# Three edge passes of a graph network: each 128-edge tile gathered once and found by registers

## The chip, the cores and the metric

The kernel runs on one core of a Trainium2 chip. The metric is the device time of one execution, in microseconds, as the median of several runs. One further execution was taken with the hardware profiler, and all rows come from that one.

## What is computed

A graph has 6250 nodes of 256 features and 100,000 edges, sorted by destination. Node numbers of destinations go as the square of a uniform number, so the first nodes have many edges each and the last ones few. Three attention steps run over the edges, with dense node work between them (cut from the reference):

```
layer 0, GAT, 4 heads:  logits = leaky_relu(a_src[src] + a_dst[dst]); alpha = softmax of logits over each dst
                        x1 = prelu(segment_sum(h[src] * alpha, dst) + bias)
layer 0, attention:     logits2 = sum(q[d2] * k[s2]) * scale; alpha2 = softmax over each d2
                        out = prelu(segment_sum(v[s2] * alpha2, d2) + x1 @ Wskip + bskip)
layer 1, typed GAT, 8 heads: alpha = leaky(xs[src] . a_s[etype] + xd[dst] . a_d[etype]); softmax over dst, times edge weight
                        out = segment_sum(xs[src] * a, dst) + bias; layernorm, feed-forward, layernorm
```

## The kernel before, in words

The program is a chain of stages with a barrier between them: `visits_and_nodes_in`, an edge pass ("gat"), `nodes_mid`, an edge pass ("attn", with `ph.dot` true), `nodes_between`, an edge pass ("typed"), `nodes_ffn`. The three edge passes are one function, `edge_pass`, called with three `Phase` objects; I call them passes one, two and three.

The 100,000 edges are cut into NT = 782 tiles of 128 edges, the 6250 destinations into 49 blocks of 128 nodes. A **visit** is a tile together with one destination block that it touches. A tile on the border of two blocks is visited twice, so there are 782 + 48 = 830 visits, filled up to VISIT_END = 832, in 52 **batches** of G = 16.

For each visit GpSimd issues one indirect DMA (line 278) that gathers the source rows of the tile's 128 edges from a table in HBM into a ring X of 48 (pass two: 40) slots in SBUF. The row numbers come from column 0 of `m.tables`, which SyncE loads batch by batch. TensorE spreads destination data over the edges through a one-hot matrix (`expand`, line 374 in pass two, 378 in the others). In passes one and three VectorE adds source and destination parts of the logits for a whole batch (`source_logits`, line 469 or 466, at the start of a batch and one batch ahead), runs a chain of scans for the running maximum of each destination, and then scales each gathered tile by its weights in place (`scale_rows`, line 591). In pass two VectorE forms a dot product per visit 25 visits ahead (`dot`, line 454), and ScalarE makes weighted one-hots (lines 307 and 313). In all passes TensorE sums a visit into PSUM (line 425), and VectorE adds that to the block's accumulator (line 613), whose place comes from a register. `rescale` (line 599 in pass two, 603 otherwise) shrinks the accumulator at a batch's start.

Order is written out by hand. Each engine runs one loop over v, with the work of each visit at fixed offsets, and semaphores between them. In VectorE's loop the order at v is: scale v + 2 (or dot v + 25), chain parts, add v - 1, more chain parts. A scaling waits until the add just before it has finished:

```
                if v >= 4:
                    dve.wait_ge(S["added"], v - 3)
                row = X[:, v % RING, 0:D].rearrange("p (h c) -> p h c", h=H)
```

VectorE loads the 16 block numbers of a batch into registers by one load per batch (line 444), TensorE four numbers per load (line 356). SyncE issues all loads of tables, one-hots, segments and joins, and waits there for buffers to come free. VectorE itself waits for gathered tiles (`landed`, in `dot` and `source_logits`), by groups of QUARTER = 4 visits. GpSimd does nothing in a pass but the gathers.

## Time and profile before

| | |
|---|---|
| median of 3 runs | 4141.51 us (4139.8 to 4142.21) |
| the profiled execution's own time | 4127.7 us |
| its span, first to last instruction | 4126.1 us |
| TensorE busy | 3059.6 us, 74% |
| VectorE busy | 3194.5 us, 77% |
| ScalarE busy | 1535.4 us, 37% |
| GpSimd busy | 2771.6 us, 67% |
| mean granted TensorE clock | 0.858 |
| first gather of passes one, two, three, at | 141.7, 1384.2, 2626.7 us |
| last gather of passes one, two, three, at | 1182.6, 2423.9, 3667.6 us |

The span is the stretch that the trace covers. "Busy" leaves out register, branch, semaphore and DMA-issuing instructions, but counts GpSimd's indirect gathers. The letter q behind an engine's name (DVEq, PEldq, SPq) stands for its sequencer, which fetches instructions, waits for semaphores and does register work. A row of the timeline gives start (us), length (us), engine, line, operation, operands and, in brackets, the engine's idle time just before and what ended it. A row of windows gives the stretch and its length, the busy us (and instructions) of TensorE, TensorE's weight loads, VectorE, ScalarE and GpSimd, the granted TensorE clock, the busy share of the DMA engines and GB/s.

### The profile page before, as it was taken

Reading aid. Unit: us, or ns where it says so; the run is one execution under the profiler, and the core shown is the slowest. Engines: PE = TensorE matmul, PEld = TensorE weight load, DVE = VectorE, ACT = ScalarE, POOL = GpSimd, SP = SyncE. Lnnn points to the kernel's source line nnn. Section 1 sums busy time; section 2 is a strip of 40 time slices with the busy share of each in tenths; the row PEclk is TensorE's granted clock in tenths of the full one; section 3 lists DMA queues with packets and bytes.
Section 4 is the critical chain, followed back from the end, with each engine's and each line's share of the span. In section 5 each row is a group of like instructions: output and inputs, shape, how many; then the busy total and the mean of one; then the engine's idle time right before and its main releaser. Section 6 shows DMA issues by size and latency. Waiting matters only on the chain. (4 is left out here: it accounts for less than half of the span.)

```text
span 4126.1 us, 67495 instructions
## 1 busy us (share of the span) xinstructions
PE 3059.6 (74%) x15494; PEld 2152.1 (52%) x15494; DVE 3194.5 (77%) x11152; ACT 1535.4 (37%) x3947; POOL 2771.6 (67%) x3112
## 2 busy tenths in 40 slices
PE   6467677766667688778788779577777777768998
PEld 4344445444446455455555546344444444447887
DVE  6577888777787677777777769688888888887665
ACT  2333333333328466666666656211111111113332
POOL 3577777777730477777777745677777777746776
PEclk8778887788879799999999989788788888789999
DMA  7655555555534444444444436555555555532221
GB/s 144 176 168 166 167 167 168 170 173 168 167 82 131 137 136 140 139 137 137 137 137 137 139 96 221 186 157 159 156 157 156 156 159 160 152 85 89 66 66 46
DMA packets 297058, 586.64 MB, mean 142 GB/s; under 512 B 89485, under 2 KB 186777, under 8 KB 296746
## 3 DMA queue, kind: packets, MB, share of 16 engines
q0 software_dynamic: 123184, 355.57, 31.4%
q1 hardware_dynamic: 141434, 197.50, 16.0%
q10 hardware_dynamic: 32128, 29.99, 2.4%
q8 instruction: 126, 2.06, 0.2%
q14 instruction: 186, 1.52, 0.1%
HBM read 505.09 MB, written 77.73 MB: 141 GB/s over the span
## 5 line engine op out<-in xcount | busy, mean ns | idle before, releaser
L425 PE MATMUL psum<-big,onehots_or_distances 128*128 128x264 f32 (+2 forms) x4992 | 1885.5, 488 | 149.7 <-ACT onehots_or_distances L313 86.2
L613 DVE TENSOR_TENSOR acc<-acc,psum 128x264 f32 (+2 forms) x2496 | 1062.8, 426 | 259.1 <-PE psum L425 153.5
L425 PEld LDWEIGHTS psum<-big,onehots_or_distances 128*128 128x128 f32 x4992 | 937.1, 228 | 433.3 <-issue 167.7
L278 POOL DMA_INDIRECT big<-table_attn,tables x832 | 787.4, 946 | 453.8 <-DMA tables<-edge_tables 200.7
L278 POOL DMA_INDIRECT big<-table_typed,tables x832 | 788.7, 948 | 264.3 <-issue 194.6
L278 POOL DMA_INDIRECT big<-table_gat,tables x832 | 788.7, 948 | 263.7 <-issue 187.4
L334 ACT ACTIVATE onehots_or_distances<-psum 128x512 f32<-128x512 f32 x416 | 248.6, 597 | 1630.9 <-PE psum L388 1570.4
L591 DVE TENSOR_TENSOR big<-big,psum 128x256 f32<-128x256 f32 x1664 | 679.7, 414 | 26.9 <-ACT psum L299 1.4
L378 PE MATMUL psum<-big 128*128 x1664 | 279.4, 196 | 453.5 <-DVE raw L479 228.1
L374 PE MATMUL psum<-big,onehot_t 128*128 x2496 | 456.0, 294 | 113.9 <-DVE raw L454 102.0
L454 DVE CUSTOM_DVE_ANT_0 junk<-psum,big 128x258 f32<-128x258 f32 x832 | 346.2, 417 | 197.4 <-DMA big<-table_attn,tables 185.8
L378 PEld LDWEIGHTS psum<-big 128*128 128x128 bf16 x1664 | 187.3, 114 | 591.2 <-issue 520.7
L307 ACT ACTIVATE onehots_or_distances<-iota,tables 128x128 f32<-128x128 f32 x832 | 330.5, 397 | 386.7 <-DVE acc L613 376.8
L374 PEld LDWEIGHTS psum<-big,onehot_t 128*128 128x128 bf16 x2496 | 258.1, 104 | 305.4 <-issue 184.6
L313 ACT ACTIVATE onehots_or_distances<-onehots_or_distances,weight,neg_weight 128x128 f32<-128x128 f32 x832 | 397.6, 478 | 0.0
L388 PEld LDWEIGHTS psum<-ident,big 128*128 128x128 bf16 x1664 | 157.6, 116 | 102.9 <-issue 44.0
L1698 ACT ACTIVATE big<-psum,big 128x128 f32<-128x128 f32 x392 | 106.7, 383 | 258.2 <-PE psum L1737 258.2
L400 PE MATMUL psum<-growth,ones 64*128 64x4 f32 (+2 forms) x312 | 63.2, 272 | 180.5 <-DVE growth L566 180.5
L388 PE MATMUL psum<-ident,big 128*128 128x128 bf16 x1664 | 196.4, 252 | 0.0
L1737 PEld LDWEIGHTS psum<-big 128*128 128x128 f32 x1568 | 186.6, 195 | 5.9 <-ACT big L1690 3.4
L1737 PE MATMUL psum<-big 128*128 128x128 f32 x1568 | 187.1, 279 | 2.8 <-ACT big L1690 2.8
L773 POOL TENSOR_TENSOR big<-big,half 128x1 f32<-128x1 f32 x147 | 101.7, 692 | 117.5 <-DVE big L768 113.7
(265 smaller groups left out, 3959.8 us busy)
## 6 DMA issues: line engine op xcount, KB each, us to landing
big<-visit_positions SPq DMA_DIRECT2D x52, 512.0 KB
onehots<-big SPq DMA_DIRECT2D x52, 512.0 KB
onehot_t<-onehots SPq DMA_DIRECT2D x52, 512.0 KB
big<-onehots SPq DMA_DIRECT2D x52, 512.0 KB, 3.7
big<-table_gat,tables POOLq DMA_INDIRECT x832
big<-table_attn,tables POOLq DMA_INDIRECT x832
big<-table_typed,tables POOLq DMA_INDIRECT x832
big<-in_x_dram SPq DMA_DIRECT2D x98, 128.0 KB, 2.4
```

Of the source, the lines that this page charges most:

```text
L278: pool.indirect_dma_start(X[:, v % RING, :], None, ph.table, bass.IndirectOffsetOnAxis(ap=column(k, 0)[:, g:g + 1].bitcast(I32), axis=0)). ...
L307: nc.scalar.activation(m.dist[:, v % 4, :], m.iota[:, :], ACT.Abs, scale=-1.0, bias=column(k, 1)[:, g:g + 1]).then_inc(S["distance"], 1)
L313: nc.scalar.activation(m.onehots[:, v % 4, :], m.dist[:, v % 4, :], ACT.Relu, scale=m.neg_weight[:, k % 2, g:g + 1], bias=m.weight[:, k % ...
L334: nc.scalar.activation(m.onehots[:, at:at + 4, :], turned_onehots.rearrange("p (v n) -> p v n", n=P), ACT.Copy).then_inc(S["onehots"], 1)
L374: last = nc.tensor.matmul(ps[:, exp_banks[v % 3], 0:K], spreading, ph.tab[:, bass.ds(blk, 1), s, :].rearrange("p a k -> p (a k)"), start=( ...
L378: last = nc.tensor.matmul(expanded_at(g), spreading, ph.tab[:, bass.ds(blk, 1), :, :].rearrange("p a s k -> p (a s k)"), start=True, stop= ...
L388: last = nc.tensor.matmul(turned_onehots[:, i * P:(i + 1) * P], onehot_t(k)[:, g * P:(g + 1) * P], m.ident16[:, :], start=True, stop=True)
L425: nc.tensor.matmul(sum_ps(v), onehot_at(v), X[:, v % RING, 0:ph.WS], start=True, stop=True).then_inc(S["summed"], 1)
L454: nc.vector.tensor_tensor_reduce(out=m.junk[:, v % 3, 0:K], in0=ps[:, exp_banks[v % 3], 0:K], in1=X[:, v % RING, 0:K], scale=1.0, scalar=0 ...
L591: nc.vector.tensor_tensor(row, row, spread(row_weights[:, g, :], D // H), ALU.mult).then_inc(S["scaled"], 1)
L613: nc.vector.tensor_tensor(row, row, sum_ps(v), ALU.add).then_inc(S["added"], 1)
L1737: last = nc.tensor.matmul(ps[:, 2 + 2 * (p % 2) + f // 4, (f % 4) * P:(f % 4 + 1) * P], w1_t[:, c, f * P:(f + 1) * P], uT[:, p % 2, c * P: ...
```

## The change

Each tile is gathered once: 782 gathers a pass and not 832. The visits find their tile by a ring slot that is held in a register. Its parts:

- GpSimd walks over tiles t, with row numbers from `m.src`, which stays in SBUF for the whole program. The ring has 44 slots. Before every fourth gather GpSimd waits for the semaphore `freed`.
- SyncE no longer issues loads in a pass. It waits for each group of four tiles to land, adds to a semaphore `arrived`, and, nine groups behind, waits for the last visit of a group and adds to `freed`. So a group's gathers start only after the group two before it has landed.
- ScalarE takes over the loads that SyncE issued (`transfers`), at fixed places of its loop. In passes one and three it also copies the columns behind the 256 features of each visit's tile to a buffer `m.tails` (`copy_tails`, 31 visits ahead), after it has waited for `arrived`.
- VectorE reads `m.tails` in `source_logits`, scales from the ring slot into a second ring Y of 32 visits, and loads 16 slots per batch in addition to the 16 block numbers. In pass two its dot product reads the slot by register and doesn't wait for the landing.
- TensorE in pass two waits for `arrived` before it expands each fourth visit, 26 visits ahead, and loads four slots per four visits for its sums.
- A table of blocks, slots, needed tiles and last visits is made in the first stage. The tables of passes one and three have 260 and 272 columns, before 264 and 288.
- `tensor_tensor_reduce` in `dot` becomes `scalar_tensor_tensor` with the same accumulator output.

```diff
+RING = 44
+YR = 2 * G
+LAG = 9
...
+    def slots_of(engine, v, n):
+        at = v // G * RECORD + v % G
+        return nc.values_load_multi_w_load_instructions(
+            m.index[32:33, at:at + n], engines=[engine], min_val=0, max_val=RING - 1,
...
+            for q in range(NTQ):
+                f = q - LAG
+                last = None
+                if 0 <= f < NTQ - groups:
+                    last = sp.value_load(m.index[64:65, f:f + 1], min_val=1, max_val=VISIT_END)
+                sp.wait_ge(S[f"rows{q % groups}"], 16 * (q // groups * QUARTER + min(QUARTER, NT - q * QUARTER)))
+                sp.sem_inc(S["arrived"], QUARTER)
+                if last is not None:
+                    sp.wait_ge(S["summed" if ph.dot else "scaled"], last)
+                    sp.sem_inc(S["freed"], 1)
+
+        @block.gpsimd
+        def _(pool):
+            for t in range(NT):
+                if t >= RING and t % QUARTER == 0:
+                    pool.wait_ge(S["freed"], t // QUARTER - groups + 1)
+                pool.indirect_dma_start(X[:, t % RING, :], None, ph.table,
+                                        bass.IndirectOffsetOnAxis(ap=m.src[:, t:t + 1], axis=0)).then_inc(S[f"rows{t // QUARTER % groups}"], 16)
...
+            def copy_tails(v):
+
                 k, g = divmod(v, G)
-                if g == 0:
-                    pool.wait_ge(S[f"tables{k % TB}"], (k // TB + 1) * 16)
-                if v >= RING:
-                    pool.wait_ge(S["summed"], v - RING + 1)
...
+                if g == 0 and k >= 2:
+                    act.wait_ge(S["with_high"], k - 1)
+                if g % QUARTER == 0:
+                    act.wait_ge(S["arrived"], needs[g // QUARTER])
+                nc.scalar.activation(tails_at(k)[:, g, :], X[:, bass.ds(slots[g], 1), D:D + T].rearrange("p a w -> p (a w)"), ACT.Copy).then_inc(S["tails"], 1)
...
                 if ph.dot:
+                    if v % QUARTER == 0:
+                        pe.wait_ge(S["arrived"], need_of(PE_ENGINE, v)[0])
                     if v >= 3:
                         pe.wait_ge(S["dotted"], v - 2)
...
-                    nc.tensor.matmul(sum_ps(v), onehot_at(v), X[:, v % RING, 0:ph.WS], start=True, stop=True).then_inc(S["summed"], 1)
+                    if ph.dot and v % 4 == 0:
+                        slots = slots_of(PE_ENGINE, v, 4)
+                    rows = tile_at(slots[v % 4], ph.WS) if ph.dot else Y[:, v % YR, :]
+                    nc.tensor.matmul(sum_ps(v), onehot_at(v), rows, start=True, stop=True).then_inc(S["summed"], 1)
...
-                row = X[:, v % RING, 0:D].rearrange("p (h c) -> p h c", h=H)
-                nc.vector.tensor_tensor(row, row, spread(row_weights[:, g, :], D // H), ALU.mult).then_inc(S["scaled"], 1)
+                row = tile_at(slots[g], D).rearrange("p (h c) -> p h c", h=H)
+                nc.vector.tensor_tensor(Y[:, v % YR, 0:D].rearrange("p (h c) -> p h c", h=H), row, spread(row_weights[:, g, :], D // H), ALU.mult).then_inc(S["scaled"], 1)
...
+                u = v + (DOT_AHEAD if ph.dot else 1)
+                if 0 <= u < VISIT_END and u % G == 0:
+                    slots = ()
+                    slots = slots_of(DVE_ENGINE, u, G)
```

Three places show how the instructions now stand. ISA is a register operation of the sequencer. The first is VectorE in pass three, from the last adds of a batch over the next batch's first source logits. Before (L613 add, L579 edge weights, L591 scaling, L466 source logits, L444 block numbers):

```order
L613 ISA
L613 TENSOR_TENSOR acc<-acc,psum 128x272
L579 TENSOR_TENSOR psum<-psum,tables 128x128
L591 TENSOR_TENSOR big<-big,psum 128x256 x2
L613 ISA
L613 TENSOR_TENSOR acc<-acc,psum 128x272
L591 TENSOR_TENSOR big<-big,psum 128x256
L466 TENSOR_TENSOR both<-big,psum 128x256
L444 TENSOR_LOAD blocks
L613 ISA
L613 TENSOR_TENSOR acc<-acc,psum 128x272
```

And with the change (L663 add, L629 edge weights, L641 scaling):

```order
L663 ISA
L663 TENSOR_TENSOR acc<-acc,psum 128x272
L227 TENSOR_LOAD index
L629 TENSOR_TENSOR psum<-psum,tables 128x128
L641 ISA
L641 TENSOR_TENSOR big<-big,psum 128x256
L641 ISA
L641 TENSOR_TENSOR big<-big,psum 128x256
L663 ISA
L663 TENSOR_TENSOR acc<-acc,psum 128x272
L641 ISA
L641 TENSOR_TENSOR big<-big,psum 128x256
```

A second register load, L227, now stands before the edge weights, and every scaling has a register operation in front of it.

The second is TensorE in pass two, where a group of four visits begins. Before (L374 expand, L425 sum):

```order
L425 MATMUL psum<-big,onehots_or_distances 128x258
L356 TENSOR_LOAD blocks
L374 ISA
L374 MATMUL psum<-big,onehot_t 128x258
L374 ISA
L374 MATMUL psum<-big,onehot_t 128x258
L374 ISA
L374 MATMUL psum<-big,onehot_t 128x258
L425 MATMUL psum<-big,onehots_or_distances 128x258
```

With the change (L403 block numbers, L233 needed tile, L423 expand, L477 sum):

```order
L403 TENSOR_LOAD index
L233 TENSOR_LOAD index
L233 ISA x2
L423 ISA
L423 MATMUL psum<-big,onehot_t 128x258
L423 ISA
L423 MATMUL psum<-big,onehot_t 128x258
L423 ISA
L423 MATMUL psum<-big,onehot_t 128x258
L477 ISA
L477 MATMUL psum<-big,onehots_or_distances 128x258
```

and further on, at the first sum of a group of four:

```order
L227 TENSOR_LOAD index
L477 ISA
L477 MATMUL psum<-big,onehots_or_distances 128x258
```

Expanding now stands behind one more register load and two register operations, with the wait for `arrived` on the first L423. The sum reads its tile's place from a register, and one in four has a load in front.

The third is ScalarE in pass three with the change, behind the exponentials of a batch (L317 copies tails, L370 copies one-hots, L298 and L299 are the loads of segments and joins, L227 and L237 load slots and needs). Before, nothing stood there but the copy of the one-hots:

```order
L317 ACTIVATE dot_products<-big 128x16
L298 DMA seg<-visit_segments 128x1x385
L299 DMA joins<-visit_joins 4x128
L317 ISA
L317 ACTIVATE dot_products<-big 128x16
L370 ACTIVATE onehots_or_distances<-psum 128x512
L227 TENSOR_LOAD index
L237 TENSOR_LOAD index
L237 ISA x8
L317 ISA
L317 ACTIVATE dot_products<-big 128x16
L317 ISA
```

Two DMA issues, tail copies and the register loads now stand in ScalarE's queue between the exponentials and later copies of one-hots.

## Rows read from the trace of the kernel before

**Rows 1.** Windows in steady parts of passes one, two, three (columns below).

```profile
300.00:1100.00 800.00, 558.29 (x2707) 387.55 (x2706) 631.32 (x2185) 267.01 (x359) 605.33 (x640) 0.80 0.57 169
1500.00:2300.00 800.00, 637.84 (x3362) 416.18 (x3360) 598.14 (x2605) 499.12 (x1402) 605.01 (x641) 0.94 0.49 138
2700.00:3500.00 800.00, 581.04 (x2711) 381.85 (x2710) 698.07 (x2313) 127.16 (x279) 605.37 (x640) 0.82 0.56 157
```

**Rows 2.** Gathers of pass three by line: min/median/max ns, first and last start.

```profile
L278 POOL DMA_INDIRECT big<-table_typed,tables x832: 942/946/1131, 2626.7 to 3667.6; - x167
```

**Rows 3.** Batch cadence by line: first source-logit addition of passes one and three.

```profile
L469 DVE TENSOR_TENSOR raw<-big,psum x52: 253/261/265, 163.5 to 1186.9; 128x64 f32<-128x64 f32 x52
...
L466 DVE TENSOR_TENSOR both<-big,psum x52: 414/422/423, 2648.5 to 3671.9; 128x256 f32<-128x256 f32 x52
```

**Rows 4.** Waits of VectorE at 200:1180, 1400:2420, 2650:3660 us; total us, times, longest.

```profile
DVE raw L469 <- DMA big<-table_gat,tables: 79.0, 27, 5.5
DVE acc L613 <- PE psum L425: 69.4, 124, 1.9
DVE acc L613 <- issue: 34.9, 31, 2.1
...
DVE junk L454 <- DMA big<-table_attn,tables: 184.9, 103, 4.5
...
DVE acc L613 <- PE psum L425: 46.4, 90, 1.1
DVE both L466 <- DMA big<-table_typed,tables: 38.0, 37, 8.1
DVE acc L613 <- issue: 33.0, 39, 1.1
```

**Rows 5.** Register loads by line, on the sequencers of VectorE and TensorE.

```profile
L444 DVEq TENSOR_LOAD <-blocks x156: 1092/1099/2333, 183.4 to 3691.0; - x156
...
L356 PEldq TENSOR_LOAD <-blocks x624: 325/332/1832, 138.9 to 3661.8; - x156
```

**Rows 6.** Timeline of VectorE in pass three, round one batch boundary.

```profile
2803.42 0.43 DVE L613 TENSOR_TENSOR acc<-acc,psum 128x272 f32 x1
2803.89 0.42 DVE L591 TENSOR_TENSOR big<-big,psum 128x256 f32<-128x256 f32 x1
2804.23 0.43 DVE L613 TENSOR_TENSOR acc<-acc,psum 128x272 f32 x1
...
2808.98 0.42 DVE L466 TENSOR_TENSOR both<-big,psum 128x256 f32<-128x256 f32 x1 [0.67 <-DMA big<-table_typed,tables]
2810.26 0.44 DVE L613 TENSOR_TENSOR acc<-acc,psum 128x272 f32 x1 [0.85 <-issue]
```

**Rows 7.** Timeline of VectorE in pass two; then the rescaling line on its sequencer.

```profile
1903.37 0.42 DVE L613 TENSOR_TENSOR acc<-acc,psum 128x258 f32 x1 [0.78 <-issue]
1904.01 0.44 DVE L599 TENSOR_SCALAR acc<-acc,shrink  x1 [0.21 <-DVE acc L613]
...
L599 DVEq FUSED_REGOPS  x52: 57/57/65, 1422.3 to 2440.9; - x52
```

**Rows 8.** Waits of TensorE at 1400:2420 us; total us, times, longest.

```profile
PE psum L374 <- DVE raw L454: 94.2, 57, 3.2
PE psum L425 <- ACT onehots_or_distances L313: 83.7, 206, 1.1
```

**Rows 9.** Timeline of a gather on GpSimd and the product that waited, pass two.

```profile
1903.38 0.95 POOL L278 DMA_INDIRECT big<-table_attn,tables  x1 [0.30 <-issue]
...
1908.18 0.43 DVE L454 CUSTOM_DVE_ANT_0 junk<-psum,big 128x258 f32<-128x258 f32 x1 [2.38 <-DMA big<-table_attn,tables]
```

**Rows 10.** Timeline at the start of pass three, GpSimd and the SyncE queue.

```profile
2624.45 0.81 SPq L227 DMA_DIRECT2D tables<-edge_tables  x2
2626.68 1.07 POOL L278 DMA_INDIRECT big<-table_typed,tables  x1 [11.23 <-DMA tables<-edge_tables]
```

**Rows 11.** Timeline of ScalarE in pass three.

```profile
2805.87 0.22 ACT L292 ACTIVATE psum<-psum,first_hot 128x8 f32<-128x8 f32 x1
```

More of the change, by code:

```diff
@@ L132, with __init__ @@
 class Phase:
-    def __init__(self, m, name, heads, table, width, summed, keys, ring):
+    def __init__(self, m, name, heads, table, width, summed, keys):
         self.name, self.H, self.R = name, heads, heads * G
@@ L150 @@
 LEAD = 2 * G
-QUARTER = 4
 TB = 5
@@ L157, in edge_pass @@
 def edge_pass(nc, m, dram, ph):
-    H, R, X, K, RING = ph.H, ph.R, ph.X, ph.keys, ph.ring
+    H, R, X, Y, K, T = ph.H, ph.R, ph.X, ph.Y, ph.keys, ph.tails
     RQ = max(R, 32)
@@ L198, in onehot_t, with scaled_at, tails_at, tile_at @@
     def onehot_t(k):
-        return m.onehot_t[:, k % 2, :] if ph.dot else m.hot_ring.bitcast(BF16)[:, k % HOT, :]
+        if ph.dot or k % HOT >= 4:
+            return m.onehot_t[:, k % 2, :]
+        return m.hot_ring.bitcast(BF16)[:, k % HOT, :]
     turned_onehots = ps[:, 7, 0:4 * P]
-    def rows_at(k):
-        at = k * G % RING
-        return X[:, at:at + G, :]
+    def scaled_at(k):
+        return Y[:, k % 2 * G:(k % 2 + 1) * G, :]
+    def tails_at(k):
+        return m.tails[:, k % 2, :, 0:T]
+    def tile_at(slot, width):
+        return X[:, bass.ds(slot, 1), 0:width].rearrange("p a w -> p (a w)")
+    def slots_of(engine, v, n):
+        at = v // G * RECORD + v % G
+        return nc.values_load_multi_w_load_instructions(
+            m.index[32:33, at:at + n], engines=[engine], min_val=0, max_val=RING - 1,
+            skip_runtime_bounds_check_because="a tile's place in the ring is its number modulo the ring")[1]
+    def need_of(engine, v):
+        at = v // G * RECORD + G + v % G // QUARTER
+        return nc.values_load_multi_w_load_instructions(m.index[32:33, at:at + 1], engines=[engine], min_val=1, max_val=NT)[1]
+    def needs_of(engine, k):
+        at = k * RECORD + G
+        return nc.values_load_multi_w_load_instructions(m.index[32:33, at:at + 4], engines=[engine], min_val=1, max_val=NT)[1]
     with ExitStack() as ctx:
@@ L210, in edge_pass @@
         block = ctx.enter_context(nc.Block())
-        def landed(eng, v):
-            eng.wait_ge(S[f"rows{v // QUARTER % groups}"], (v // RING + 1) * QUARTER * 16)
         def batch_at(v):
@@ L286, in weigh @@
                 if not ph.dot:
-                    nc.scalar.activation(rows_at(k)[:, :, D:D + H], by_visit(shifted), ACT.Exp).then_inc(S["denominators"], 1)
+                    nc.scalar.activation(scaled_at(k)[:, :, D:D + H], by_visit(shifted), ACT.Exp).then_inc(S["denominators"], 1)
                 if k:
@@ L336, in _ @@
             weigh_at = G - 1 if ph.dot else G - 2
-            for v in range(-3 * G, VISIT_END):
+            slots = needs = ()
+            for v in range(-5 * G, VISIT_END):
+                transfers(v)
                 if ph.dot and 0 <= v + 1 < VISIT_END:
@@ L351, in _ @@
                         transposed_onehot(v // G + 3)
+                u = v + 2 * G - 1
+                if not ph.dot and 0 <= u < VISIT_END:
+                    if u % G == 0:
+                        slots = needs = ()
+                        slots, needs = slots_of(ACT_ENGINE, u, G), needs_of(ACT_ENGINE, u // G)
+                    copy_tails(u)
+            if ph.name == "gat":
+                for i in range(HOT):
+                    act.wait_ge(S[f"onehot_stored{i}"], 16 * ((NBATCH - i + HOT - 1) // HOT))
         @block.tensor
@@ L459, in source_logits @@
                 dve.wait_ge(S["expanded"], k + 1)
-                for q in range(0, G, QUARTER):
-                    landed(dve, k * G + q)
+                dve.wait_ge(S["tails"], (k + 1) * G)
                 if ph.typed:
@@ L778, in visits_and_nodes_in @@
     v_, n_ = Space(m.acc), Space(m.big[:, 0:16384])
-    rec = [v_.take(4 * P).bitcast(I32) for _ in range(VC)]
+    rec = [v_.take(3 * P).bitcast(I32) for _ in range(VC)]
     wrec = [v_.take(P) for _ in range(VC)]
@@ L790, in visits_and_nodes_in @@
     rel16 = [n_.take(P // 2).bitcast(BF16) for _ in range(2)]
-    scal = [n_.take(4) for _ in range(2)]
+    scal = [n_.take(3) for _ in range(2)]
     KB = NV // G
```

208 lines of the change are left out of this document (114 added, 94 removed).

## The prediction

> **What bounds the kernel now.** I first read the windows in the steady part of each pass [rows 1]. VectorE is the busiest engine in passes one and three (631 and 698 of 800 us), TensorE in pass two, and GpSimd shows the same 605 us in all three. That sameness is the clue. Each gather takes 946 ns [rows 2] and stands 0.30 us behind the one before it [rows 9]: GpSimd never stops, whatever the pass. From its first to its last gather, pass three takes (3667.6 - 2626.7) / 831 = 1.253 us per visit [rows 2], 20.04 us per batch of 16. The first addition of source logits comes every (1186.9 - 163.5) / 51 = 20.07 us in pass one and every (3671.9 - 2648.5) / 51 = 20.07 us in pass three [rows 3]. So GpSimd's gathers set the pace of all three passes, and the gap of 0.30 us is part of a gather's price.
>
> The waits then tell how far away the next bound is. VectorE waits for gathered tiles for 79.0 us over 980 us (49 batches) in pass one, 184.9 over 1020 us (51) in pass two and 38.0 over 1010 us (50) in pass three [rows 4]. Per batch that is 1.6, 3.6 and 0.75 us. Without these waits VectorE's own batch would take about 18.4, 16.4 and 19.3 us. Whatever a faster gather brings, a pass can't fall below that.
>
> **What the gathers give.** 50 gathers of 832 go, at 1.253 us: 62.6 us a pass if GpSimd stays the bound. It isn't spread evenly. Destinations crowd into the first blocks, so the first seven batches still need 16 tiles each, the mean is 782 / 52 = 15.0 (18.8 us), and the last batches need 14 (17.5 us). A narrower row changes nothing, since the price is one of issuing.
>
> The passes also start earlier. In pass three SyncE issues the table load at 2624.45 and the first gather follows at 2626.68, having waited for it [rows 10]. With the row numbers already in SBUF that 2.2 us goes, three times: -7 us, because the first batches wait for gathers anyway.
>
> **What it costs VectorE.** Two things are added in its queue.
> First, a second load of 16 registers per batch. The existing one takes 1099 ns [rows 5]. The add behind it starts 1.28 us after the logit addition, where two neighbours are otherwise 0.34 us apart [rows 6], so 0.94 us of it is bare. The new one stands, in passes one and three, behind the last adds of a batch, where the trace shows no idle engine time to hide it beyond what TensorE causes. I take 0.95 us a batch. Bounds are 0 (if it falls wholly into a wait) and 1.1.
> Second, a register operation in front of each scaling, behind the wait for the add just finished. Now a scaling starts 0.04 us after that add's end (2803.85 to 2803.89) [rows 6]. The nearest case with wait and register operation is the rescaling: it starts 0.21 us after the add's end, with one further semaphore wait in front, and its register operation takes 57 ns [rows 7]. So the price per scaling lies between 0.06 and 0.17 us. I take 0.11, because the rescaling has the extra wait. Of 16 scalings, eight (pass three: six, and the edge weights pass it to one more) stand directly behind an add; for the others a chain part lies between and hides most. That makes 1.2 us a batch in pass one and 1.0 in pass three.
> Some of this is given back. VectorE also waits for TensorE's sums: 69.4 + 34.9 = 104 us in pass one and 46.4 + 33.0 = 79 us in pass three [rows 4], of which 0.94 us a batch is the existing register load. That leaves 1.2 and 0.6 us a batch. A slower VectorE finds the sums sooner. I give back half, 0.6 and 0.3.
> VectorE's batch then is 18.4 + 0.95 + 1.2 - 0.6 = 19.95 us in pass one, 19.3 + 0.95 + 1.0 - 0.3 = 20.95 in pass three. In pass two the products have their wait and register work ahead of the engine, and the load costs 0.95: 16.4 + 0.95 + 0.3 for late expansions = 17.65, just above what the last batches ask of GpSimd and below all others. `scalar_tensor_tensor` with an accumulator output I cost at no change against the 430 ns of the old product [rows 9].
>
> **Sum by pass.**
> Pass one: the first batches stay at 20.04 us by gathers, the others go from 20.05 to 19.95: 49 x -0.05 = -2 us. The last two batches have no gathers beside them, and the added queue work is bare there: +3. With the start -2: -1 us.
> Pass two: -63 by gathers, -2 at the start, +1 at the end, and +6 that I allow for TensorE's added queue work and the tighter ring (below): -58 us.
> Pass three: 49 x (20.95 - 20.05) = +44, +3 at the end, -2 at the start: +45 us.
> The node stages gain and lose a few short instructions, which I cost at 0.
> Together -14 us, against the profiled execution's 4127.7 us: 4114. The median of the runs shown is 14 us above that execution, so the median should be 4141.5 - 14 = 4127.5, say **4128 us**. A difference of 0.2% (8 us) is about what a measurement can tell from no change.
>
> **Other moved work.** ScalarE's tail copies: its shortest activation takes 0.22 us [rows 11], and with a register operation I take 0.3, 16 times 5 us a batch. With two register loads (1.1 and 0.33 [rows 5]), eight register operations and four or five DMA issues of about 0.4 us (two take 0.81 us on SyncE [rows 10]) some 9 us are added. ScalarE is busy for 267 of 800 us in pass one and 127 in pass three [rows 1], 6.7 and 3.2 us a batch, so it stays at 16 and 12 of 20 us. Its load costs nothing; its order may (first rival).
> The wait in pass two moves from VectorE's product, behind which the adds queue, to TensorE's expansion, behind which the sums queue, and the adds behind those. Since arrivals go on meanwhile, this only shifts work later as long as the ring has room. A gather ends at 1904.33 and the product that waited for it starts at 1908.18 [rows 9], 3.9 us later; I take 4 us for a slow landing. A group of gathers may start only when the one two before has landed, with 4 x 1.25 = 5 us of issuing between: enough. VectorE needs tiles 29 to 32 visits ahead out of 44 slots freed in fours; what is left for jitter is about 3 us.
> TensorE in pass two gets, per group of four visits, a load of one number with two register operations before it can expand, and a load of four (0.33 us [rows 5]) behind the wait for the weighted one-hot. It waits for that one-hot 206 times in 204 groups, 83.7 us [rows 8], so once per group this load may lie bare: at most 0.45 us, in all perhaps 0.8 us per group of 4.4 to 5 us. Its busy time is 638 of 800 us [rows 1], 4.0 us a group. That is full, but the clock stood at 0.94 there and it waits for VectorE for another 94.2 us, waits that were caused by missing tiles [rows 8].
> On such loads the Trainium skill speaks against the change: the page "DMA: Bandwidth & Descriptors", section "Latency and other measured facts", gives a `tensor_load` a floor of about 600 ns. This trace disagrees, at 332 ns for four numbers and 1099 for sixteen. By the page's floor TensorE's two new loads would come to 1.2 us a group, 4.8 us a batch on top of 16, and pass two would lose its gain, as in rival (b).
>
> **The rivals.**
> (a) *ScalarE's order holds VectorE up: slower.* The batch's exponentials, the last tail copies, two DMA issues, the register loads and a wait for `arrived` stand in one queue. VectorE's source logits need all 16 tails. If that queue reaches them later than VectorE, each batch of passes one and three stretches by the difference. It decides once ScalarE's stretch from shifted logits to last tail (about 1 us of exponentials, 3 x 0.3, 2 x 0.4 of issues: 2.7 us) exceeds VectorE's two adds, load and three scalings (about 3.5 us). With 0.8 us more a batch: 100 x 0.8 = +80, 4208 us. For it: the margin is under 1 us. Against: ScalarE is idle for most of its time.
> (b) *TensorE becomes the bound in pass two: slower.* The loads lie bare each time, and the pass keeps its 20.0 us a batch. The -58 is gone: 4186 us. For it: 4.0 + 0.8 us against 4.4 in the last groups. Against: its clock can rise and its waits shrink.
> (c) *VectorE's added queue work hides: faster.* If load and register operations fall into waits for TensorE and into the chain, passes one and three run at 18.9 and 19.4 us, -56 and -33, and pass two keeps -58: 3995 us. For it: 1.2 and 0.6 us of waits a batch. Against: they are shorter than 2.15 and 1.95 us of added work.
> (d) *The change doesn't do what it says.* That the gathers stay at 832 is excluded by the loop over 782 tiles. But if the gap of 0.30 us grows, say by waits for `freed`, the gain shrinks; this lies within the forecast's range.
>
> **How the numbers follow.** The forecast, gain in pass two and loss in pass three with pass one even, gets 0.50; its own range is 4095 to 4170, from 0.06 or 0.17 us per scaling and from a TensorE allowance between 0 and 20. (a) gets 0.24, (b) 0.12, (c) 0.14. The range of 4045 to 4225 leaves out most of (c), where nearly everything hides, and the far end of (a). Faster by over 0.2%: (c) and 0.32 of the forecast, 0.46. Within 0.2%: 0.11 of the forecast. Slower: (a), (b) and the forecast's upper end, 0.43.
>
> **What would show it.** GpSimd: 782 gathers a pass at 1.25 us, without long waits in pass two, but with waits for SyncE's `freed` in passes one and three. Pass two some 58 us shorter; the source logits of pass three every 20.9 us, of pass one every 20.0, early batches included. VectorE's scaling starting some 0.15 us behind its add, and two register loads per batch with about 0.95 us bare behind each. The forecast is wrong if VectorE waits for tails (a), if TensorE in pass two has no waits for tiles left (b), or if pass three is shorter than 1041 us of gathers (c).

## The result

| | before | changed |
|---|---|---|
| median | 4142.21 us (4139.8 to 4143.94, 5 runs) | 4158.7 us (4154.61 to 4165.21, 5 runs) |
| span of the profiled execution | 4126.1 us | 4152.6 us |
| first stage | 135.6 us | 147.8 us |
| pass one | 1080.4 us | 1082.8 us |
| pass two | 1071.3 us | 1034.3 us |
| pass three | 1082.3 us | 1130.0 us |
| the three other stages together | 753.4 us | 754.7 us |
| VectorE, ScalarE busy | 3194.5, 1535.4 us | 3238.0, 1745.1 us |
| granted TensorE clock, mean | 0.858 | 0.859 |

The ratio is 1.0043, with a 95% interval of 1.0028 to 1.0057: slower by 0.4%, where the forecast was faster by 0.3%. The stages are read from barrier to barrier in the two traces; between the two profiled executions the changed kernel is 26.5 us longer, between the medians 16.5.

The windows of the changed kernel in the steady parts of the passes, to be held against [rows 1]:

```profile
300.00:1100.00 800.00, 580.09 (x2720) 390.17 (x2720) 645.22 (x2200) 338.58 (x1000) 576.15 (x609) 0.81 0.57 162
1500.00:2300.00 800.00, 659.83 (x3505) 434.41 (x3504) 635.45 (x2711) 524.81 (x1458) 605.50 (x639) 0.95 0.50 139
2700.00:3500.00 800.00, 574.85 (x2604) 371.07 (x2602) 681.59 (x2226) 201.99 (x879) 556.46 (x587) 0.81 0.51 140
```

GpSimd has 605 us of 800 only in pass two now. In passes one and three it has become slack, and the gathers (here by line: duration min/median/max, first and last start) no longer set the pace there:

```profile
L266 POOL DMA_INDIRECT big<-table_gat,src_by_edge x782: 940/947/1059, 151.7 to 1174.5; - x196
L266 POOL DMA_INDIRECT big<-table_attn,src_by_edge x782: 941/947/1087, 1397.8 to 2380.7; - x196
L266 POOL DMA_INDIRECT big<-table_typed,src_by_edge x782: 941/947/1067, 2603.3 to 3671.7; - x196
```

Pass two takes 983 us from its first to its last gather, pass three 1068 for the same number. The source logits, the lines that answer to [rows 3]:

```profile
L517 DVE TENSOR_TENSOR raw<-dot_products,psum x52: 252/254/263, 179.7 to 1197.3; 128x64 f32<-128x64 f32 x52
...
L514 DVE TENSOR_TENSOR dot_products<-dot_products,psum x52: 411/411/422, 2627.5 to 3695.6; 128x256 f32<-128x256 f32 x52
```

That is 19.95 us a batch in pass one and 20.94 in pass three, where the forecast had 19.95 and 20.95. GpSimd's waits for a place in the ring (windows 200:1180, then 2650:3660; us, times, longest) show who is behind:

```profile
POOL big L266 <- SPq L259: 63.6, 64, 3.4
...
POOL big L266 <- SPq L259: 113.2, 83, 4.2
```

VectorE's timeline in pass three, at two scalings behind adds and at a batch boundary:

```profile
2864.30 0.43 DVE L663 TENSOR_TENSOR acc<-acc,psum 128x272 f32 x1
2864.87 0.42 DVE L641 TENSOR_TENSOR big<-big,psum 128x256 f32<-128x256 f32 x1
2865.21 0.43 DVE L663 TENSOR_TENSOR acc<-acc,psum 128x272 f32 x1
...
2855.75 0.44 DVE L663 TENSOR_TENSOR acc<-acc,psum 128x272 f32 x1 [0.21 <-DVE acc L663]
2856.92 0.30 DVE L629 TENSOR_TENSOR psum<-psum,tables 128x128 f32<-128x128 f32 x1 [0.73 <-issue]
```

From add to scaling it is 0.57 us now and was 0.47 [rows 6]. Over all 318 such scalings of pass three the median gap between the end of the add and the start of the scaling went from 0.035 to 0.143 us, and over the 420 of pass one from 0.034 to 0.143: 0.109 us each, where the forecast took 0.11. Where another instruction lies between, the scaling used to start 0.08 us before the end of that one; now it starts 0.04 before in pass three and 0.01 before in pass one (medians; behind some chain parts it now starts 0.05 behind the end). The second row pair shows the new load of 16 numbers: VectorE's sequencer is at it from 2855.78 to 2856.87, and the edge weights, whose inputs ScalarE had ready at 2856.1, start behind it.

### The profile page after: what moved, and what is told of

Read it like the earlier page. It is cut to its first block and busy times, and to the rows that moved or that the text cites. A ratio compares the mean times of both kernels' runs of the same rounds, so it can differ in the third digit from the quotient of the medians.

```text
span 4152.6 us, 78881 instructions
## 1 busy us (share of the span) xinstructions
PE 3103.5 (75%) x15488; PEld 2157.0 (52%) x15488; DVE 3238.0 (78%) x11147; ACT 1745.1 (42%) x5611; POOL 2633.4 (63%) x2962
## 5 line engine op out<-in xcount | busy, mean ns | idle before, releaser
L477 PE MATMUL psum<-big,onehots_or_distances 128*128 128x264 f32 (+2 forms) x4992 | 1931.4, 495 | 201.6 <-DVE big L641 72.6
L663 DVE TENSOR_TENSOR acc<-acc,psum 128x264 f32 (+2 forms) x2496 | 1058.7, 424 | 246.4 <-PE psum L477 193.5
L477 PEld LDWEIGHTS psum<-big,onehots_or_distances 128*128 128x128 f32 x4992 | 934.2, 228 | 514.0 <-issue 363.3
L266 POOL DMA_INDIRECT big<-table_attn,src_by_edge x782 | 742.5, 949 | 463.7 <-issue 235.9
L266 POOL DMA_INDIRECT big<-table_typed,src_by_edge x782 | 741.7, 948 | 337.3 <-issue 212.1
L266 POOL DMA_INDIRECT big<-table_gat,src_by_edge x782 | 741.6, 948 | 290.4 <-issue 218.5
L641 DVE TENSOR_TENSOR big<-big,psum 128x256 f32<-128x256 f32 x1664 | 685.1, 417 | 173.7 <-DVE acc L663 40.2
L370 ACT ACTIVATE onehots_or_distances<-psum 128x512 f32<-128x512 f32 x416 | 248.5, 597 | 1069.3 <-PE psum L437 1051.5
L423 PE MATMUL psum<-big,onehot_t 128*128 x2496 | 445.8, 290 | 147.8 <-DVE dot_products L504 83.0
L504 DVE SCALAR_TENSOR_TENSOR dot_products<-psum,big 128x258 f32<-128x258 f32 x832 | 347.5, 418 | 112.0 <-PE psum L423 108.6
L423 PEld LDWEIGHTS psum<-big,onehot_t 128*128 128x128 bf16 x2496 | 255.0, 102 | 337.9 <-issue 223.5
L317 ACT ACTIVATE dot_products<-big 128x4 f32 (+1 forms) x1664 | 250.8, 202 | 407.2 <-issue 294.6
L427 PE MATMUL psum<-big 128*128 x1152 | 194.9, 196 | 238.2 <-DVE dot_products L524 107.4
L427 PEld LDWEIGHTS psum<-big 128*128 128x128 bf16 x1152 | 130.7, 115 | 336.0 <-issue 290.3
L449 PEld LDWEIGHTS psum<-growth,ones 64*128 64x128 f32 (+2 forms) x312 | 48.6, 195 | 262.1 <-DVE growth L616 261.8
L1824 PE MATMUL psum<-big 128*128 128x256 f32 x784 | 177.2, 379 | 0.0
```

What stands on the lines that cost most here:

```text
L266: pool.indirect_dma_start(X[:, t % RING, :], None, ph.table, bass.IndirectOffsetOnAxis(ap=m.src[:, t:t + 1], axis=0)).then_inc(S[f"rows{t ...
L317: nc.scalar.activation(tails_at(k)[:, g, :], X[:, bass.ds(slots[g], 1), D:D + T].rearrange("p a w -> p (a w)"), ACT.Copy).then_inc(S["tail ...
L423: last = nc.tensor.matmul(ps[:, exp_banks[v % 3], 0:K], spreading, ph.tab[:, bass.ds(blk, 1), s, :].rearrange("p a k -> p (a k)"), start=( ...
L427: last = nc.tensor.matmul(expanded_at(g), spreading, ph.tab[:, bass.ds(blk, 1), :, :].rearrange("p a s k -> p (a s k)"), start=True, stop= ...
L477: nc.tensor.matmul(sum_ps(v), onehot_at(v), rows, start=True, stop=True).then_inc(S["summed"], 1)
L504: nc.vector.scalar_tensor_tensor(m.junk[:, v % 3, 0:K], ps[:, exp_banks[v % 3], 0:K], 1.0, tile_at(slots[v % G], K), ALU.mult, ALU.mult, a ...
```

## The experiments

Each kernel was timed beside the kernel before on its chip: 4130 us for all but one group, which is told of at the end. "Second half" is the cadence of the last 24 to 26 batches, where the gathers have 15 tiles and fewer to fetch, so that it shows what the engines need. The rows for it, from source logits by line in a window, are given where a verdict hangs on them. Lengths of passes come from one profile each. Where an experiment leaves a pass as in the changed kernel (needs_once counts as such), pass one took 1082.8 to 1089.8 us, pass two 1030.8 to 1034.6 and pass three 1118.0 to 1133.8, so a smaller difference than these spreads tells nothing.

**static_load and static_noload: the scaling without its register.**

```
-  row = tile_at(slots[g], D)...
-  tensor_tensor(Y[:, v % YR, 0:D]..., row, ...)
+  row = Y[:, v % YR, 0:D]...
+  tensor_tensor(row, row, ...)
```

> Leaves out the reading of the gathered rows in passes one and three: the scaling multiplies what lies in its own slot of Y, at a fixed address, so no register operation stands in front of it. The second register load of VectorE stays. Theory one (register operation behind the add's completion stretches VectorE's batch): pass three goes from 20.9 to about 19.9 us a batch, some 50 us off its 1130 us; pass one from 19.9 to about 18.9, some 40 us off its 1083. Theory two (ScalarE's queue or the ring of tiles holds the pass): both passes keep their length within 10 us. Pass two unchanged.

Measured: 4008.04 us, ratio 0.9698 (0.9682 to 0.9715); passes one and three at 1031.5 and 1042.2. It leaves out that the gathered rows are read, so it scales its own old values. The gain is larger than expected, 51 and 88 us. But the trace has 208 register loads of VectorE and not 312: nothing used the second load's results, and the compiler had dropped it. So this kernel takes away both additions, and static_noload (4011.34 us, ratio 0.9703), which was to take away the load as well, is the same program in what matters. The two tell that both additions together are what costs passes one and three, and nothing about either.

**fixed_load: the load without the register operations.** The same, but each batch's last visit reads its tile by register, which keeps the load.

> static_load with VectorE's load of 16 places really kept: in passes one and three every scaling works in a fixed place, but that of each batch's last visit reads its tile by its register, which keeps the load in the program (in static_load the compiler had dropped it, since nothing used it: 208 loads of VectorE in its trace, 312 in the changed kernel's). If the register operations are the price, passes one and three stay within 5 us of static_load's 1031 and 1042. If the load is, they come back toward the changed kernel's 1083 and 1130: by its full 1.10 us a batch, 57 us each, up to 1080 and 1100. From the trace of the changed kernel (0.73 us bare ahead of the edge weights in pass three) I expect 1043 to 1060 in pass three and 1031 to 1045 in pass one, where the gathers give it cover.

Measured: 4068.46 us, ratio 0.9855 (0.9838 to 0.9871); pass one 1052.5, pass three 1077.7. The load costs more than expected. How much is best seen with the next kernel.

**before_3of4_again: what the engines of the kernel before need.** Without the gather of every fourth visit:

```
+  if v % QUARTER == QUARTER - 1:
+      continue
   pool.indirect_dma_start(X[:, v % RING, :], None, ph.table, ...)
```

> The kernel before without the gather of every fourth visit, whose place in the ring holds zeros, once more; it leaves out a quarter of the rows. Gathers then take 15 us of a batch, and the batches show what the other engines need. By the prediction's own estimates (18.4, 16.4 and 19.3 us in a batch): passes of 970 to 990, 870 to 890 and 1010 to 1030 us. Rival (those estimates counted waits of the engines for one another as time that falls away without gathers): 18.6 to 20 us in a batch, passes of 980 to 1050 us each, pass two among them at 960 to 1010.

Measured: 3796.31 us (one run), passes of 978.6, 901.7 and 1015.7; pass two is 12 us above the expected range, the others are within it. The source logits of pass three in the second half, of this kernel, of fixed_load and of the changed kernel:

```profile
L468 DVE TENSOR_TENSOR both<-big,psum x24: 411/411/420, 2886.9 to 3322.4; 128x256 f32<-128x256 f32 x24
```

```profile
L514 DVE TENSOR_TENSOR dot_products<-dot_products,psum x25: 411/411/412, 3108.7 to 3585.0; 128x256 f32<-128x256 f32 x25
```

```profile
L514 DVE TENSOR_TENSOR dot_products<-dot_products,psum x25: 411/411/415, 3168.4 to 3674.9; 128x256 f32<-128x256 f32 x25
```

Divided by 23, 24 and 24 batches: 18.93, 19.85 and 21.10 us. The first step, 0.92 us, is the load; the second, 1.25 us, the register operations. The first of these kernels is also without all the rest of the change, but that costs VectorE nothing here: static_load has the rest of the change and neither of the two, and its line

```profile
L514 DVE TENSOR_TENSOR dot_products<-dot_products,psum x26: 414/414/421, 3081.2 to 3554.1; 128x256 f32<-128x256 f32 x26
```

gives 18.92 us over 25 batches. In pass one the same three kernels give 18.21, 19.17 and 19.97 us: 0.96 and 0.80.

**two_loads: a load more.**

```
   slots = slots_of(DVE_ENGINE, u, G)
+  if not ph.dot:
+      more = slots_of(DVE_ENGINE, u + 1, G - 1)
+      slots = slots[0:1] + more
```

> The changed kernel with one more load of VectorE in each batch of passes one and three, behind the existing one: 16 places, then the same from the second on, and both are used. If a load is bare where VectorE is what binds: 1.0 to 1.1 us a batch, +52 to +57 us in each of the two passes, 4260 to 4275 us in all. If it falls into the wait for the new weights: pass three is within 15 us of 1130, pass one within 15 of 1083.

Measured: 4516.79 us, ratio 1.0936 (1.0918 to 1.0955), far beyond both expectations. Passes one and three take 1275.6 and 1300.5 us. One pair of its loads in pass three, and VectorE's timeline there:

```profile
L227 DVEq TENSOR_LOAD <-index x2: 1100/2251/3402, 2906.6 to 2907.7; - x2
```

```profile
2906.56 0.44 DVE L663 TENSOR_TENSOR acc<-acc,psum 128x272 f32 x1 [1.07 <-PE psum L477]
2911.17 0.30 DVE L629 TENSOR_TENSOR psum<-psum,tables 128x128 f32<-128x128 f32 x1 [4.17 <-issue]
```

The second load takes 3.40 us, three times the first, though it fetches 15 numbers and not 16; it starts one number further on. Pass three goes from 21.10 to 24.30 us a batch, so 3.2 of the 3.4 us are bare. So nothing covers a load at this place.

**late_wait: the register operation's cover.** It keeps load and registers, moves the scaling's wait back by one add and gives every add a wait for the add before it.

```
-  if v >= 4:
-      dve.wait_ge(S["added"], v - 3)
+  if v >= 5:
+      dve.wait_ge(S["added"], v - 4)
...
-  elif ph.dot or v >= VISIT_END - 3 or v % G == G - 3:
+  else:
       dve.wait_ge(S["added"], v)
```

> The kernel of late_wait once more, since the chip of its first run timed even the kernel before at 4738 us. The scaling of a visit waits for the add before last instead of the last one, so that its register operation and its start no longer lie behind VectorE's own add; every add waits for the add before it; nothing else is changed. Theory one (the register operation behind the wait is the cost): passes one and three come down as with the fixed address, to 1030 to 1040 and 1040 to 1055 us, against 1083 and 1130 in the changed kernel, and the whole to 4010 to 4035 us. Theory two (the fixed address saved because the scaling no longer read and wrote two places of memory): passes one and three stay within 10 us of the changed kernel's, and the whole at 4140 to 4160 us. Pass two: within 5 us of 1034 by both.

Measured: 4022.59 us, ratio 0.9734 (0.9714 to 0.9754); passes one and three 1034.5 and 1051.8. Theory one holds. Its timeline in pass three:

```profile
2861.96 0.43 DVE L663 TENSOR_TENSOR acc<-acc,psum 128x272 f32 x1
2862.31 0.41 DVE L641 TENSOR_TENSOR big<-big,psum 128x256 f32<-128x256 f32 x1
2862.64 0.43 DVE L663 TENSOR_TENSOR acc<-acc,psum 128x272 f32 x1
```

The scaling starts 0.35 us after the add started and 0.08 before it ends: 0.22 us earlier than in the changed kernel, and 0.11 earlier than in the kernel before, though the register operation is still there. Once nothing makes the sequencer wait for the instruction just ahead, it does the register work while that one runs. GpSimd now waits 12.2 and 29.4 us in these passes for places in the ring, where it had 63.6 and 115.5 in the whole of each, so the gathers set most of the pace again.

**dve_waits_again: who waits in pass two.** The wait for `arrived` goes back from TensorE's expansion to VectorE's product, with one load of four needed tile numbers a batch.

> The kernel of dve_waits once more: in pass two VectorE, and not TensorE, waits for the tiles to arrive; the rest is the changed kernel. Theory one (who waits matters, since VectorE's products are behind a wait of its own): pass two takes 1045 to 1065 us instead of 1034, the whole 4170 to 4190 us. Theory two (pass two is set by the gathers while a batch has 16 tiles, and by the round through TensorE and VectorE after that, and no tile is late): pass two stays within 5 us of 1034, the whole within 10 us of the changed kernel's.

Measured: 4185.37 us, ratio 1.0127 (1.01 to 1.0153), pass two 1062.1. By its number, 28 us, theory one holds. The trace points to another reason than the wait. The two leading waits of VectorE's products in pass two:

```profile
DVE dot_products L504 <- issue: 103.5, 43, 2.9
...
DVE dot_products L504 <- SPq L256: 21.4, 18, 2.7
```

The products stand idle 43 times in 51 batches, 2.4 us each: once a batch VectorE's sequencer is at its load of 16 numbers (1.10 us), that of the four needed ones (0.34) and their four register operations and checks (1.1). Arrivals themselves are waited for 21.4 us. By these rows it is mostly the queue work that comes with the wait, and not the wait, that is dear on VectorE; no run has the one without the other. On TensorE three of four such loads could go without an effect (needs_once, below).

**dot_fixed, sum_fixed, both_fixed: what holds pass two.** Products (VectorE), sums (TensorE) or both read a fixed place of zeros, and TensorE's loads of places go in the second and third. They leave out the gathered rows of pass two in products, sums or both.

> Three edits of the changed kernel, one in each pass, so that each is read from its own pass. Pass two: VectorE's products read one fixed place of zeros instead of the gathered tile, so that no register operation lies ahead of them (its logits are then zero); the 16-number load stays. If the register operation costs pass two what it cost the others, the late batches fall from 18.85 us to 17 to 18 (gathers allow some 18.0) and the pass from 1034 to 1005 to 1020; if not, both stay. Pass one: a third 16-number load of VectorE in each batch. If a load costs its 1.10 us where VectorE is what binds, pass one is 40 to 57 us longer than 1083; if it falls into a wait, it stays within 5. Pass three: a tile's place is given back eight groups after it arrived, not nine, so that SyncE waits earlier for the scalings before it announces the next group. If SyncE's order costs time, pass three is 10 us or more above 1130; if not, within 5.

> The changed kernel, but in pass two TensorE's sums read one fixed place of zeros, and TensorE loads no places; VectorE's products still read the gathered tiles (pass two's sums are then zero). Theory one (TensorE's loads and register addresses lengthen the round through TensorE and VectorE in pass two): late batches fall from 18.85 to 17 to 18 us, the pass from 1034 to 1005 to 1020. Theory two (they lie in time in which TensorE waits anyway): the pass stays within 5 us of 1034.

> The changed kernel with both edits in pass two: products and sums from one fixed place, no load of places by TensorE; the wait for arrived tiles and VectorE's load stay. If these two edits are all that the change adds to the engines' work in pass two, its late batches go down to what the gathers allow, some 18.0 us and less at the end, and the pass to 990 to 1010. If the late batches stay above 18.5, what holds them is neither: then it is the wait for arrived tiles, or VectorE's load.

Measured, pass two: dot_fixed 1024.6, sum_fixed 1020.3, both_fixed 1015.4, against 1034.3 (one run each; the whole 4144.95, 4145.85 and 4124.9 us). Each of the first two has a part, 10 and 14 us, and both fall short of the expected 1005 to 1020; together they give 19, short of 990 to 1010. The unchanged pass two lies between 1030.8 and 1034.6, so the parts may be as little as 6 and 10. By the count of loads in the traces, VectorE's load in pass two was dropped in dot_fixed and in both_fixed as well, since nothing used its numbers, so VectorE's part is that of load and register operations together. The extra load that dot_fixed was to have in pass one was dropped too and tells nothing; its third edit, giving places back eight groups after arrival and not nine, left pass three at 1131.6, so no cost of SyncE's order shows. The waits of TensorE in pass two of both_fixed:

```profile
PE psum L424 <- SPq L257: 116.7, 73, 12.5
PE psum L424 <- DVE dot_products L503: 69.7, 112, 4.2
```

TensorE waits for arrivals 116.7 us against 63.0 in the changed kernel, and in the second half (window 1950:2420) 25.7 us against 6.9. So with both edits the gathers again hold up more of the late batches; TensorE's wait for VectorE's products, 34.3 us there, is still the longer one.

**needs_once, t0_full, x_first: no effect.** TensorE loading its four needed tile numbers once per batch (ratio 1.0042, 1.0026 to 1.0059; pass two 1034.6), the rows of the first table kept at 264 numbers (1.0041, 1.0026 to 1.0055), and SyncE's last five loads of x ahead of its wait for the places (1.0046, 1.0029 to 1.0063) all leave the changed kernel where it was (1.0043).

> In pass two TensorE loads the four tile numbers that it waits for once per batch, in one load, in place of four loads of one number each. Theory one (TensorE's queue work of about 0.5 us per group of four visits bounds the later batches at 18.8 us): three of four such pieces go, the later batches come to about 17.7 us, pass two loses 25 to 40 us of 1034. Theory two (VectorE's products or the tiles bound it): pass two stays within 5 us. The other passes unchanged.

> The table of pass one is stored and gathered with 264 columns again and not 260, ring slots included. Theory one (shorter rows land later, and ScalarE waits for the stores): the first stage, 147.8 us from the first barrier to the second, comes down by 6 to 10 us. Theory two (the added chain of small VectorE instructions for the places, or the load of row numbers at the head of ScalarE's queue, costs the 12 us): it stays within 2 us. Passes unchanged within 5 us.

The last was aimed at the first stage:

> The changed kernel with SyncE issuing the loads of the last five blocks of x before it waits for the places, not behind the places' way to memory and back; the rest is the same. Theory one (the first stage is 12 us longer because these five loads are issued at 135.1 to 137.5 us instead of 121.4 to 123.7): the first stage takes 138 to 142 us instead of 147.8, the whole is 6 to 10 us less than the changed kernel's, 4143 to 4150 us. Theory two (the rows of the table of pass one are stored more slowly, and the loads are only late because everything is): the first stage stays within 2 us of 147.8.

The first stage took 146.6 us, and in t0_full 147. For x_first this is theory two: the loads were late because everything was. For t0_full, whose range of 2 us it meets too, it takes the row's width out as the cause, as far as one profile and the ratio can tell.

**all_three: the version that beats both.** late_wait, needs_once and t0_full together.

> A version for use: late_wait (the scaling waits for the add before last, every add for the add before it), needs_once (TensorE loads a batch's four needed tile numbers at once) and t0_full (the table of pass one has whole rows of 264) together. Since needs_once and t0_full alone moved nothing, 4015 to 4030 us where before takes 4130, ratio 0.972 to 0.976. If either of them helps now that the passes are set by the gathers, down to 4005.

Measured: 4015.51 us (4014.5 to 4019.47, 5 runs) where the kernel before took 4130.21, ratio 0.972 (0.9706 to 0.9733). It is 2.8% faster than before, on that chip. That it beats late_wait_again alone isn't shown; their intervals overlap.

**A chip of its own.** The first runs of late_wait, dve_waits and before_3of4, and the one of double_load, fell on a chip on which the kernel before took 4738.39 us (4733.13 to 4742.73, 7 runs), 15% more than on the others. They took 5091, 5053, 4161 and 5077 us. double_load's extra load had been dropped by the compiler too, so it is the changed kernel, and 5077 (one run) is what that takes there: 7% more than before. late_wait's ratio there is 1.0741 (1.0712 to 1.0769), so the gain that it shows on the other chips is absent on this one. The gathers took their usual time (mean 949 ns), but in the first 60 us of pass one, and again near the start of pass three, ScalarE's register operations ahead of the copies of tails came to 0.7 us instead of 0.055. By line, in late_wait on that chip and in late_wait_again:

```profile
L317 ACTq FUSED_REGOPS  x1664: 8/55/1394, 165.0 to 4630.0; - x185
```

```profile
L317 ACTq FUSED_REGOPS  x1664: 55/55/60, 164.7 to 3566.2; - x185
```

34 of ScalarE's were over 0.5 us. That is too little for 1000 us, and the kernel before, without them, is slow there as well. The trace of before_3of4 on this chip has more of something else: idle time of TensorE for which it shows no reason. The entry that grew most, and the same in before_3of4_again:

```profile
PEld psum L427 <- issue: 361.3, 567, 25.7
```

```profile
PEld psum L427 <- issue: 169.3, 409, 2.4
```

In the variants of the changed kernel there GpSimd waits 355 to 402 us a pass for places in the ring, and the other engines wait for tiles, each for the other. What starts it stays open, and no verdict on the other chips rests on these runs.

## Why the prediction was wrong, and where it was right

Right: *what bounds the kernel now*. Gathers at 1.253 us each, the gap of 0.30 us included, set all passes before. In pass two they go on at that pace in the changed kernel: GpSimd waits there only 5.4 us for places, near the end. The engines' own batches, forecast as 18.4, 16.4 and 19.3 us from waits alone, came out as 18.2, 16.6 and 18.9 once gathers were scarce.

Right: *what it costs VectorE*. The load at 0.95 us was 0.96 and 0.92. The register operations at 1.2 and 1.0 us were 0.80 and 1.25; the price of one behind an add, 0.11, was 0.109, but in pass three more of the others paid a share than "hides most" allowed (0.04 to 0.12 us each behind five of the eight kinds of instruction that stand there), and in pass one the batch grew by less than the gaps did, so some fell into waits. What I had given back (0.6, 0.3) was there in pass one, and not in pass three; that the start of pass three's sum (19.3) was 0.4 too high made up for it, which is luck. So pass one (-1 forecast, +2.4 measured) and pass three (+45, +47.7) stand. A slip in the sum changes little: 20.05 and 19.95 are 0.10 apart, not the 0.05 that was taken 49 times, so pass one's term should have been some 2 us lower.

Wrong, first: the term of pass two, -58 us, measured -37.0. The gathers gave what they should: their span fell from 1039.7 to 982.9 us, 57 less, where the forecast had 63 less the 6 allowed to TensorE. But from the last gather to the last add it is 49.3 us and was 28.2: 21 more, where the sum has "+1 at the end". The step that failed is "16.4 + 0.95 + 0.3 for late expansions = 17.65", the pace from which it follows that the engines keep up with the late gathers. The products of the second half (lines of the changed kernel, of both_fixed and of before_3of4_again):

```profile
L504 DVE SCALAR_TENSOR_TENSOR dot_products<-psum,big x381: 375/420/429, 1949.9 to 2398.8; 128x258 f32<-128x258 f32 x191
```

```profile
L503 DVE SCALAR_TENSOR_TENSOR dot_products<-psum,fixed x364: 375/418/428, 1951.4 to 2369.7; 128x258 f32<-128x258 f32 x182
```

```profile
L456 DVE CUSTOM_DVE_ANT_0 junk<-psum,big x374: 376/417/427, 1750.7 to 2138.7; 128x258 f32<-128x258 f32 x187
```

Per batch of 16: 18.90, 18.44 and 16.64 us. The gathers would allow the middle one, so the first is set by the engines for the most part, and the change has put up to 2.3 us on a batch's own time, not 1.25. While a batch has 16 tiles nobody sees it; when it has 14, at 17.5 us, the engines fall behind the gathers and pay at the end. I had said that products "have their wait and register work ahead of the engine". But taking VectorE's load and register operations away brings 10 us, taking TensorE's brings 14, and both together 19 of the 21 missing. The likely way is that VectorE and TensorE hand three PSUM banks back and forth, so that work in either's sequencer lengthens that round; no run tests the banks. Rival (b) had seen TensorE's loads, but the pass kept 37 of its 58 us. TensorE's loads are short, 0.33 us for four numbers and 0.31 for one, and needs_once shows that three of four of those for needed tiles cost nothing. The Trainium skill's page "DMA: Bandwidth & Descriptors", section "Latency and other measured facts", gives a `tensor_load` a floor of about 600 ns. These traces disagree, with 0.31 and 0.33 us.

Wrong, second: "the node stages gain and lose a few short instructions, which I cost at 0". The first stage is 12.2 us longer in the profile. Over the profiles of the changed kernel and of those experiments that leave the first stage as it is, it takes 143.7 to 150.6 us; the kernel before and before_3of4_again take 135.6 and 138.4. The loss starts early: the store of the thirteenth of 49 blocks of the first table goes out at 61.0 us where it was 55.2, the thirty-first at 111.0 where it was 103.0, and the last at 147.6 where it was 135.4. ScalarE waits for rows of that table to be stored, 43.7 us where it was 33.2:

```profile
ACT big L980 <- DMA table_gat<-big: 43.7, 14, 5.9
```

Neither the row width (t0_full) nor the late loads of x (x_first) are the cause. The added chain of places was not tried by itself; the cause stays open.

By passes: -1, -58, +45 and 0 were forecast, +2.4, -37.0, +47.7 and +12.2 measured, and +1.3 in the other stages. These add up to the 26.5 us between the two profiled executions; between the medians it is 16.5, so some 10 us of them belong to the executions and not to the change. The two wrong terms, 33 us together, turned a small gain into a small loss. The rivals (a) and (c) did not come: VectorE waits for tails at the start of a pass alone, and of its added work little hides, in pass three next to nothing.

What the forecast lacked most is not a term but a look one step further. It priced the register operation behind a wait at 0.11 us and left it there. The wait itself, for the instruction just ahead, was worth as much again, and giving it one instruction of slack turned the changed kernel's 0.4% over the kernel before into 2.7% below it. What the same slack would do in the kernel before, where the gathers set the pace, was not run.

## What to carry to other kernels

When a faster resource uncovers another engine, list that engine's waits for its own previous instruction: each was hidden here while the engine had slack. A wait that can be met by the instruction before last lets the sequencer do register work under the running one (0.35 us from start to start here, against 0.57). And check in the trace that an experiment's added instruction is there: four of these kernels (static_load, double_load, dot_fixed, both_fixed) had lost a load to the compiler, and only the count of loads told.

## What was not expected of the hardware

A register load of 15 numbers that starts one number behind the usual place took 3.40 us, where 16 numbers take 1.10; whether the start or the length does it was not tried. One chip ran the kernel before 15% slower than the others. Of it no profile was taken there; in before_3of4, which was profiled on both, the gathers took the same 0.95 us and the node stages after pass one 163, 174 and 419 us on either chip, while the three passes were 117, 178 and 73 us longer.
